# Moving one group of matmuls earlier in TensorE's order, and cutting another into single blocks, in a two-layer transformer kernel

## Chip, cores and metric

The kernel runs on one core of a Trainium2 chip. The metric is the device time of one execution in microseconds (us), the median of the runs. The engines of a core are TensorE (PE in the profile; its weight loads are PEld), VectorE (DVE), ScalarE (ACT), GpSimd (POOL) and SyncE (SP), which here issues the DMAs.

## The reference

Two transformer blocks with adaptive layer norm, on x of 8 batch elements x 512 tokens x 128 channels. The change lies in the attention of the second block (16 heads of width 8). What is computed there, shortened:

```python
qkv = (x @ w_qkv.T + b_qkv)                      # q, k, v: [B, H, T, 8]
std_logits = einsum('bhqd,bhkd->bhqk', q, k) * scale
write_lines = exterior(w1, w2); read_lines = exterior(r1, r2)   # 6 numbers per token and head
incidence = einsum('bqhp,bkhp->bhqk', read_lines, J_write)
weights = decays[:, None, None] ** diffs_pos[None] * past[None]
logits = std_logits + incidence * weights[None] * bias_scale
logits = where(causal_mask, -inf, logits)        # key after query: out
attn = softmax(logits); out = einsum('bhqk,bhkd->bqhd', attn, v)
return out @ w_out.T + b_out
```

## The kernel before, in words

The program runs as stages: preparation, attention and feed-forward of block 0, then `attention1` (the function `attention1` holds all that the change touches; 491 to about 1015 us of the span), then the feed-forward of block 1.

In `attention1` there are 8 x 16 = 128 heads, numbered n. The 512 tokens are NT = 4 tiles of 128, so the causal scores of a head are 4 blocks on the diagonal and 6 below it (key tile k before query tile a). Every head is computed twice. First with queries on the partitions, only to find the largest score of each query; then, LAG = 8 heads later (j = n - 8), with keys on the partitions, with the maxima subtracted through three more rows of the operands, and these scores go through the exponential and on to the product with v. The rows QO (queries) and KA (keys, with decay), KB, KC (for the diagonal) lie in SBUF in a ring of four groups of four heads and come from DRAM scratch by DMA.

Each engine runs its own loop over n = 0 ... 151, and the order within a turn ("slot") is written out by hand. TensorE's turn:

1. `on_diagonal(n)` (L1299, L1300, and the mask matmul L1301), after VectorE's `weigh(n)`
2. in three slots of four (n mod 4 = 1, 2, 3, from head 13 on) `values` of an earlier group of four heads (L1356, fp32, 32 columns of the array each), in the fourth `turn_out` (L1364, transposes); once per batch element `turn_rows` and `project` (L1377, L1383)
3. `incidences_by_key(j)` (L1316): eight matmuls of 64 columns into bank psDT, after s_expd of head j-1
4. `side(n)`: a step of the operands of a later batch element (L1079 to L1115), in most slots
5. `below(n)` (L1308): the blocks below the diagonal into psX, after VectorE has read the maxima of head n-1 (s_rc)
6. `incidences(n+1)` (L1292) into psD
7. `on_diagonal_by_key(j)` (L1323 to L1325), after VectorE's `weigh_by_key(j)`
8. `below_by_key(j+1)` (L1333): six matmuls of 128 columns; every fourth slot `turn_maxima` (L1340)

VectorE's turn: `weigh(n)` (L1436, after L1292), `largest_below(n-1)` (L1454, L1455), `largest_on_diagonal(n)` (L1446, after L1301), `weigh_by_key(j)` (L1441, after L1316), `normalise` (L1467, L1471) every fourth slot, `residual` (L1478) once per batch element, then a step of its side work (L1121 to L1154). ScalarE's turn: a side step, copies of the output (L1575, every fourth slot), the exponentials of the diagonal (L1562, L1563, after L1325; the second signals s_expd), and those below it (L1557, after L1333).

The maxima of a head are gathered in mo, 4 x 4 numbers per partition: one row of four for each query tile, filled as far as there are blocks. L1460 takes the largest of each row of four.

Of the kernel before, what the change touches and what calls it, by code (L numbers as in the profile page):

```python
# [11 lines left out]
ALU = mybir.AluOpType  # L12
AX = mybir.AxisListType

P = 128
B, T, D = 8, 512, 128
NT = T // P
# [14 lines left out]
def tiles(ap, n=NT):  # L32
    return ap.rearrange("p (t c) -> p t c", t=n)


def over(ap, n):
    return ap.rearrange("p (o c) -> p o c", o=1).to_broadcast([ap.shape[0], n, ap.shape[1]])
# [12 lines left out]
class Chip:  # L50
# [9 lines left out]
    def sb(self, name, cols, dt=F32, rows=P, at=None):  # L60
        return (at or self.ctx).enter_context(self.nc.sbuf_tensor(name, [rows, cols], dt))[:, :]
# [799 lines left out]
def attention1(c, t, sh):  # L861
# [5 lines left out]
    nc, pe, dve, act, pool, sp, bank = c.nc, c.pe, c.dve, c.act, c.pool, c.sp, c.bank  # L867
    own = ExitStack()
    with own:
        sb = lambda *a, **k: c.sb(*a, at=own, **k)  # L870
        SCALE = float(DH) ** -0.5
        NR, KX = NL * H, T * (NT - 1) // 2
# [3 lines left out]
        HEADS, G, RING, LAG, NV = B * H, 4, 4, 8, 3  # L876
# [9 lines left out]
        HB = P // 2  # L886

        PAIRS = [(k, a) for k in range(NT) for a in range(k + 1, NT)]

        ROW_AT = {3: 0, 1: 512, 2: 512 + P}  # L890
        NP = len(PAIRS)
        SEG = NT + NP
        MAX_UNIT = 2.0 ** 15
        off = [P * a * (a - 1) // 2 for a in range(NT + 1)]
# [10 lines left out]
        s_inc, s_wq, s_own, s_ra, s_off, s_rb, s_rc, s_mx = c.signals("3", "inc wq own ra off rb rc mx")  # L905
# [23 lines left out]
        QO = [sb(f"QO{i}", G * T, dt=F16) for i in range(RING)]  # L929
        KB = [sb(f"KB{i}", G * T, dt=F16) for i in range(RING)]  # L930
        KC = [sb(f"KC{i}", G * T, dt=F16) for i in range(RING)]
        KA = [sb(f"KA{i}", G * KX, dt=F16) for i in range(RING)]
# [7 lines left out]
        mo = [sb(f"mo{i}", G * NT * NT) for i in range(2)]  # L940
# [10 lines left out]
        psD, psX, psDT, psXT, psO, psA = bank[0], c.banks(1, 2), bank[3], c.banks(4, 2), bank[6], bank[7]  # L951
# [9 lines left out]
        def place(n):  # L961

            return n // G % RING, n % G

        def group_at(n, after):

            q, r = divmod(n - after - G - LAG, G)
            return q if r == 0 and 0 <= q < GROUPS_ else None
# [8 lines left out]
        def rows_at(n, after):  # L977
            return next((b for b in range(B) if rows_slot(b) + after == n), None)
# [293 lines left out]
        def on_pe():  # L1272
            def block(x, n, a):

                i, h = place(n)
                return x[i][:, h * T + a * P:h * T + (a + 1) * P]
# [18 lines left out]
            def on_diagonal(n):  # L1295
                pe.wait_ge(s_wq, n + 1)
                for a in range(NT):
                    q, k = block(QO, n, a), block(KB, n, a)
                    pe.matmul(psD[HB:P, a * P:(a + 1) * P], q[:, HB:P], k, start=False, stop=False, skip_group_check=True)  # L1299
                    pe.matmul(psD[0:HB, a * P + HB:(a + 1) * P], q[:, 0:HB], k[:, 0:HB], start=False, stop=False, skip_group_check=True)  # L1300
                pe.matmul(tiles(psD), sh.identh, over(maskq, NT), start=False, stop=True, skip_group_check=True).then_inc(s_own, 1)  # L1301

            def below(n):
                if n:
                    pe.wait_ge(s_rc, n)
                i, h = place(n)
                for a, at in ROW_AT.items():
                    m = pe.matmul(psX[:, at:at + a * P], block(QO, n, a), KA[i][:, h * KX + off[a]:h * KX + off[a + 1]], start=True, stop=True, skip_group_check=True)  # L1308
                m.then_inc(s_off, 1)

            def incidences_by_key(n):
                if n:
                    pe.wait_ge(s_expd, n)
                for a in range(NT):
                    for z in HALVES:
                        m = pe.matmul(psDT[z, a * P:a * P + HB], block(KC, n, a)[:, z], block(QO, n, a)[:, z], start=a == 0, stop=False, skip_group_check=True)  # L1316
                m.then_inc(s_incT, 1)
# [24 lines left out]
            def values(q, k):  # L1342

                b = q // 4
                if k == 0:
                    pe.wait_ge(s_expd, G * (q + 1))
                    pe.wait_ge(s_expo, G * (q + 1))
                    if q:
                        pe.wait_ge(s_O, q)
                at, first = k * P, NT + sum(NT - 1 - x for x in range(k))  # L1350
                for c0, c1, e0 in ((at, at + P, at), (at + P, T, first * P)):
                    if c0 < c1:
                        for n in range(G * q, G * q + G):
                            h = n % H
                            r, v0 = 32 * (h % 4), (k * H + h) * VH
                            m = pe.matmul(psO[r:r + 32, c0:c1], vv[b % NV][:, v0:v0 + 32], ET[n % NE][:, e0:e0 + c1 - c0],  # L1356
                                          start=c0 == 0, stop=k == NT - 1, skip_group_check=True)
                if k == NT - 1:
                    m.then_inc(s_pv, 1)

            def turn_out(q):
                pe.wait_ge(s_oS, q + 1)
                for i in range(NT):
                    m = pe.transpose(psO[:, i * P:(i + 1) * P], oS[:, i * P:(i + 1) * P], sh.ident)  # L1364
                m.then_inc(s_oT, 1)

            def turn_rows(b):
                pe.wait_ge(s_O, 4 * b + 4)

                if b + 3 < B:  # L1370
                    pe.wait_ge(s_cp, 2 * (b + 3) + 2)
                else:
                    pe.wait_ge(s_rawlo, 2 * B)
                if b:
                    pe.wait_ge(s_Y, b)
                for i in range(NT):
                    m = pe.transpose(psA[:, i * P:(i + 1) * P], O[:, i * P:(i + 1) * P], sh.ident)  # L1377
                m.then_inc(s_OT, 1)
# [15 lines left out]
            for n in range(LAST):  # L1394
                j = n - LAG
                if n < HEADS:
                    on_diagonal(n)
                q = group_at(n, 1)
                if q is not None:
                    values(q, 0)  # L1400
                q = group_at(n, 2)
                if q is not None:
                    values(q, 1)
                q = group_at(n, 3)
                if q is not None:
                    values(q, 2)
                    values(q, 3)
                q = group_at(n, 4)
                if q is not None:
                    turn_out(q)  # L1410
                b = rows_at(n, 0)
                if b is not None:
                    turn_rows(b)
                b = rows_at(n, 1)
                if b is not None:
                    project(b)
                if 0 <= j < HEADS:
                    incidences_by_key(j)
                side(n)
                if n < HEADS:  # L1420
                    below(n)
                if n + 1 < HEADS:
                    incidences(n + 1)
                if 0 <= j < HEADS:
                    on_diagonal_by_key(j)
                if 0 <= j + 1 < HEADS:
                    below_by_key(j + 1)
                g, x = divmod(n - 5, G)
                if x == 0 and 0 <= g < GROUPS_:
                    turn_maxima(g)  # L1430

        def on_dve():
# [10 lines left out]
            def largest_on_diagonal(n):  # L1443
                g, x = divmod(n, G)
                dve.wait_ge(s_own, n + 1)
                dve.tensor_reduce(tiles(mo[g % 2][:, x * NT * NT:(x + 1) * NT * NT])[:, :, NT - 1], tiles(psD), AX.X, ALU.max).then_inc(s_ra, 1)  # L1446

            def largest_below(n):
                g, x = divmod(n, G)
                to = mo[g % 2][:, x * NT * NT:(x + 1) * NT * NT]  # L1450
                dve.wait_ge(s_off, n + 1)


                dve.tensor_reduce(to[:, 12:15], tiles(psX[:, 0:3 * P], 3), AX.X, ALU.max).then_inc(s_rb, 1)  # L1454
                dve.tensor_reduce(to[:, 6:11:2], tiles(psX[:, 512:512 + 3 * P], 3), AX.X, ALU.max).then_inc(s_rc, 1)  # L1455
                if x == G - 1:
                    dve.wait_ge(s_rc, n + 1)
                    if g >= 2:
                        dve.wait_ge(s_split, 5 * (g - 1))
                    dve.tensor_reduce(mx[g % 2], tiles(mo[g % 2], G * NT), AX.X, ALU.max).then_inc(s_mx, 1)  # L1460
# [73 lines left out]
            for n in range(LAST):  # L1534
                j = n - LAG
# [126 lines left out]

        on_sp()
        on_pe()
        on_dve()
        on_act()
# [324 lines left out]
```

## Time and profile before

| | |
|---|---|
| median of 3 runs | 1245.75 us (1245.54 to 1246.93) |
| the profiled execution | 1245.75 us, of which the span 1244.5 us |
| TensorE matmul busy in the span | 913.2 us (73%), 9743 matmuls |
| VectorE, ScalarE, GpSimd busy | 808.8 (65%), 573.3 (46%), 383.1 us (31%) |
| mean granted TensorE clock | 0.856 of full speed |

A row of the timeline has start, duration, engine, line, what it writes and reads, and in brackets how long the engine was idle before it and who released it. In the chain of waits a piece's duration is what it adds to the chain. Matmuls overlap, so one that lasts 0.22 us may add 0.03. Start and duration are in us.

### The profile page before, as it was taken

Reading aid. Unit: us, or ns where it says so; the run is one execution under the profiler, and the core shown is the slowest. Engines: PE = TensorE matmul, PEld = TensorE weight load, DVE = VectorE, ACT = ScalarE, POOL = GpSimd, SP = SyncE. Lnnn points to the kernel's source line nnn. Section 1 sums busy time; section 2 is a strip of 40 time slices with the busy share of each in tenths; the row PEclk is TensorE's granted clock in tenths of the full one; section 3 lists DMA queues with packets and bytes.
Section 4 is the critical chain, followed back from the end, with each engine's and each line's share of the span. In section 5 each row is a group of like instructions: output and inputs, shape, how many; then the busy total and the mean of one; then the engine's idle time right before and its main releaser. Section 6 shows DMA issues by size and latency. Waiting matters only on the chain.

```text
span 1244.5 us, 24906 instructions
## 1 busy us (share of the span) xinstructions
PE 913.2 (73%) x9743; PEld 560.9 (45%) x9743; DVE 808.8 (65%) x1873; ACT 573.3 (46%) x1044; POOL 383.1 (31%) x638
## 2 busy tenths in 40 slices
PE   3778753575663125698989898989999951989888
PEld 1344422353442013365656565656666630344344
DVE  4554537889886712778686867686777617665754
ACT  2333322232221202266656565666565642768766
POOL 0121222444432154544444536263621100011000
PEclk8898986767686555599999999999999985999999
DMA  3000000000000116152525252434342111000000
GB/s 102 9 0 1 1 19 0 1 0 1 1 0 14 45 45 161 44 154 57 154 48 138 60 146 58 129 81 109 101 106 63 28 54 40 1 18 10 9 18 18
DMA packets 70575, 63.56 MB, mean 51 GB/s; under 512 B 30492, under 2 KB 62716, under 8 KB 70456
## 3 DMA queue, kind: packets, MB, share of 16 engines
q1 hardware_dynamic: 69016, 60.59, 18.4%
q8 instruction: 81, 1.33, 0.5%
q10 hardware_dynamic: 1440, 1.33, 0.4%
q14 instruction: 38, 0.31, 0.1%
HBM read 34.02 MB, written 27.36 MB: 49 GB/s over the span
## 4 chain that ended last, share of the span: by engine, by line
PE 49%; DVE 14%; issue 10%; POOL 6%; ACT 4%; SPq 1%; DMA 1%; POOLq 0%; ACTq 0%; DVEq 0%
PE bank L1788 10%; PE bank L1356 6%; PE bank L1301 3%; PE bank L1308 3%; PE bank L1299 3%; PE bank L1333 2%; PE bank L1316 2%; PE bank L689 2%; PE bank L1292 2%; PE bank L690 2%; PE bank L1325 2%; PE bank L1323 1%; PE bank L1101 1%; ACT 4g L1853 1%; DVE 4f L1903 1%
## 5 line engine op out<-in xcount | busy, mean ns | idle before, releaser
L1562 ACT ACTIVATE ET<-bank 64x512 f32<-64x512 f32 x128 | 75.5, 590 | 107.3 <-PE bank L1325 107.3
L1788 PE MATMUL bank<-act,h 128*128 128x512 f16 x512 | 113.1, 382 | 0.0
L1557 ACT ACTIVATE ET<-bank 128x768 f32<-128x768 f32 x128 | 103.1, 805 | 3.5 <-PE bank L1333 1.2
L1890 DVE TENSOR_TENSOR act<-4f,act 128x512 f16<-128x512 f32 x96 | 66.4, 691 | 56.8 <-ACT act L1843 56.6
L1436 DVE TENSOR_TENSOR bank<-bank,W 128x256 f32<-128x256 f32 x128 | 54.8, 428 | 72.3 <-PE bank L1292 72.3
L1441 DVE TENSOR_TENSOR bank<-bank,WT 128x256 f32<-128x256 f32 x128 | 55.2, 431 | 62.9 <-PE bank L1316 62.9
L1446 DVE TENSOR_REDUCE mo<-bank 128x4 f32<-128x512 f32 x128 | 88.1, 688 | 9.7 <-PE bank L1301 4.7
L1356 PE MATMUL bank<-ET,vv 128*32 128x128 f32 (+2 forms) x1792 | 90.9, 329 | 0.8 <-DVE O L1471 0.8
L1299 PE MATMUL bank<-KB,QO 128*64 128x128 f16 x512 | 55.0, 233 | 42.2 <-DVE bank L1436 42.2
L1788 PEld LDWEIGHTS bank<-act,h 128*128 128x128 f16 x512 | 50.4, 99 | 60.5 <-issue 2.3
L1843 ACT ACTIVATE act<-4f 128x512 f16<-128x512 f32 x96 | 60.4, 629 | 27.7 <-DVE 4f L1903 25.7
L1454 DVE TENSOR_REDUCE mo<-bank 128x3 f32<-128x384 f32 x128 | 70.0, 547 | 0.0
L1455 DVE TENSOR_REDUCE mo<-bank 128x3 f32<-128x384 f32 x128 | 70.0, 546 | 0.0
L1308 PE MATMUL bank<-KA,QO 128*128 128x384 f16 (+2 forms) x384 | 66.8, 285 | 0.0
L136 POOL TENSOR_TENSOR rstd<-ve,neghalf 128x4 f32<-128x4 f32 x16 | 18.2, 1136 | 155.9 <-DVE ve L118 155.9
L1333 PE MATMUL bank<-QO,KA 128*128 128x128 f16 x768 | 64.4, 220 | 0.0
L1299 PEld LDWEIGHTS bank<-KB,QO 128*64 128x64 f16 x512 | 33.5, 113 | 55.2 <-DVE bank L1436 47.8
L1323 PE MATMUL bank<-QO,KB 128*64 128x128 f16 x512 | 51.7, 224 | 4.4 <-DVE bank L1441 4.2
L1333 PEld LDWEIGHTS bank<-QO,KA 128*128 128x128 f16 x768 | 54.1, 99 | 1.6
L1356 PEld LDWEIGHTS bank<-ET,vv 128*32 128x32 f32 x1792 | 44.6, 111 | 22.5 <-issue 20.7
L479 ACT ACTIVATE E<-bank,nm 128x512 f32<-128x512 f32 x32 | 22.0, 688 | 68.8 <-DVE nm L434 68.8
L1301 PE MATMUL bank<-maskq,identh 128*128 128x512 bf16 x128 | 52.5, 410 | 0.0
(315 smaller groups left out, 2309.7 us busy)
## 6 DMA issues: line engine op xcount, KB each, us to landing
QO<-scr_q SPq DMA_DIRECT2D x32, 324.0 KB
KA<-scr_a SPq DMA_DIRECT2D x32, 252.0 KB
KB<-scr_k SPq DMA_DIRECT2D x32, 168.0 KB
scr_a<-dk SPq DMA_DIRECT2D x8, 288.0 KB, 2.6
KC<-scr_k SPq DMA_DIRECT2D x32, 72.0 KB
X<-in_x SPq DMA_DIRECT2D x8, 256.0 KB, 6.5
scr_q<-std SPq DMA_DIRECT2D x8, 256.0 KB, 2.4
scr_k<-std SPq DMA_DIRECT2D x8, 256.0 KB, 2.7
```

Source lines behind the costliest of these rows:

```text
L1299: pe.matmul(psD[HB:P, a * P:(a + 1) * P], q[:, HB:P], k, start=False, stop=False, skip_group_check=True)
L1301: pe.matmul(tiles(psD), sh.identh, over(maskq, NT), start=False, stop=True, skip_group_check=True).then_inc(s_own, 1)
L1308: m = pe.matmul(psX[:, at:at + a * P], block(QO, n, a), KA[i][:, h * KX + off[a]:h * KX + off[a + 1]], start=True, stop=True, skip_group_c ...
L1333: m = pe.matmul(psXT[:, x * P:(x + 1) * P], decayed(n, k, a), block(QO, n, a), start=True, stop=True, skip_group_check=True)
L1356: m = pe.matmul(psO[r:r + 32, c0:c1], vv[b % NV][:, v0:v0 + 32], ET[n % NE][:, e0:e0 + c1 - c0], start=c0 == 0, stop=k == NT - 1, skip_gro ...
L1446: dve.tensor_reduce(tiles(mo[g % 2][:, x * NT * NT:(x + 1) * NT * NT])[:, :, NT - 1], tiles(psD), AX.X, ALU.max).then_inc(s_ra, 1)
L1454: dve.tensor_reduce(to[:, 12:15], tiles(psX[:, 0:3 * P], 3), AX.X, ALU.max).then_inc(s_rb, 1)
L1455: dve.tensor_reduce(to[:, 6:11:2], tiles(psX[:, 512:512 + 3 * P], 3), AX.X, ALU.max).then_inc(s_rc, 1)
L1557: act.activation(ET[n % NE][:, T:SEG * P], psXT[:, 0:NP * P], ACT.Exp).then_inc(s_expo, 1)
L1562: act.activation(to[0:HB, :], psDT[0:HB, :], ACT.Exp)
L1788: m = pe.matmul(to, l, r, start=n == 0, stop=n == len(todo) - 1)
L1890: dve.tensor_tensor(lo, f32_[f % 3], hi, ALU.subtract).then_inc(s_lo, 1)
```

## The change

`incidences_by_key(j)` is issued directly behind `on_diagonal(n)`, ahead of the values, the transposes and the projection, and no longer behind them. `below(n)` issues six matmuls of 128 columns, one for each block, in an order of its own (BY_ROW), instead of three of 384, 128 and 256 columns; the first four fill one PSUM bank and the last two half of the next. `largest_below` reduces 512 and 256 columns instead of 384 and 384, and the maxima go to other places within a row of mo.

```diff
@@ -886,8 +886,7 @@
         HB = P // 2
 
         PAIRS = [(k, a) for k in range(NT) for a in range(k + 1, NT)]
-
-        ROW_AT = {3: 0, 1: 512, 2: 512 + P}
+        BY_ROW = [(0, 2), (1, 2), (0, 3), (1, 3), (0, 1), (2, 3)]
         NP = len(PAIRS)
         SEG = NT + NP
         MAX_UNIT = 2.0 ** 15
@@ -1303,9 +1302,8 @@
             def below(n):
                 if n:
                     pe.wait_ge(s_rc, n)
-                i, h = place(n)
-                for a, at in ROW_AT.items():
-                    m = pe.matmul(psX[:, at:at + a * P], block(QO, n, a), KA[i][:, h * KX + off[a]:h * KX + off[a + 1]], start=True, stop=True, skip_group_check=True)
+                for x, (k, a) in enumerate(BY_ROW):
+                    m = pe.matmul(psX[:, x * P:(x + 1) * P], block(QO, n, a), decayed(n, k, a), start=True, stop=True, skip_group_check=True)
                 m.then_inc(s_off, 1)
 
             def incidences_by_key(n):
@@ -1395,6 +1393,8 @@
                 j = n - LAG
                 if n < HEADS:
                     on_diagonal(n)
+                if 0 <= j < HEADS:
+                    incidences_by_key(j)
                 q = group_at(n, 1)
                 if q is not None:
                     values(q, 0)
@@ -1414,8 +1414,6 @@
                 b = rows_at(n, 1)
                 if b is not None:
                     project(b)
-                if 0 <= j < HEADS:
-                    incidences_by_key(j)
                 side(n)
                 if n < HEADS:
                     below(n)
@@ -1443,16 +1441,14 @@
             def largest_on_diagonal(n):
                 g, x = divmod(n, G)
                 dve.wait_ge(s_own, n + 1)
-                dve.tensor_reduce(tiles(mo[g % 2][:, x * NT * NT:(x + 1) * NT * NT])[:, :, NT - 1], tiles(psD), AX.X, ALU.max).then_inc(s_ra, 1)
+                dve.tensor_reduce(tiles(mo[g % 2][:, x * NT * NT:(x + 1) * NT * NT])[:, :, 0], tiles(psD), AX.X, ALU.max).then_inc(s_ra, 1)
 
             def largest_below(n):
                 g, x = divmod(n, G)
-                to = mo[g % 2][:, x * NT * NT:(x + 1) * NT * NT]
+                to = tiles(mo[g % 2][:, x * NT * NT:(x + 1) * NT * NT])
                 dve.wait_ge(s_off, n + 1)
-
-
-                dve.tensor_reduce(to[:, 12:15], tiles(psX[:, 0:3 * P], 3), AX.X, ALU.max).then_inc(s_rb, 1)
-                dve.tensor_reduce(to[:, 6:11:2], tiles(psX[:, 512:512 + 3 * P], 3), AX.X, ALU.max).then_inc(s_rc, 1)
+                dve.tensor_reduce(to[:, 2:4, 1:3], psX[:, 0:T].rearrange("p (a k c) -> p a k c", a=2, k=2), AX.X, ALU.max).then_inc(s_rb, 1)
+                dve.tensor_reduce(mo[g % 2][:, x * NT * NT + 5:x * NT * NT + 16:10], tiles(psX[:, T:NP * P], 2), AX.X, ALU.max).then_inc(s_rc, 1)
                 if x == G - 1:
                     dve.wait_ge(s_rc, n + 1)
                     if g >= 2:
```

The functions that it calls were there before: `decayed(n, k, a)` is a block of 128 columns of KA, `block(x, n, a)` one of QO, KB or KC.

## Rows read from the trace of the kernel before

**Rows 1.** Stretches (busy us and count of each engine, clock, DMA); one wait.

```profile
core 0: us, PE busy (x) PEld busy (x) DVE busy (x) ACT busy (x) POOL busy (x), PEclk, DMA share, GB/s
525.00:985.00 460.00, 427.75 (x7162) 283.69 (x7163) 344.63 (x803) 283.65 (x516) 193.66 (x409) 0.99 0.37 97
...
PEld bank L1299 <- DVE bank L1436: 45.8, 30, 4.3
```

**Rows 2.** Groups by line (count, busy us, mean ns, idle before), 480 to 1010.

```profile
L1446 DVE TENSOR_REDUCE mo<-bank 128x4 f32<-128x512 f32 x128 | 88.1, 688 | 9.7 <-PE bank L1301 4.7
...
L1454 DVE TENSOR_REDUCE mo<-bank 128x3 f32<-128x384 f32 x128 | 70.0, 547 | 0.0
...
L1441 DVE TENSOR_TENSOR bank<-bank,WT 128x256 f32<-128x256 f32 x128 | 55.2, 431 | 62.9 <-PE bank L1316 62.9
...
L1333 PEld LDWEIGHTS bank<-QO,KA 128*128 128x128 f16 x768 | 54.1, 99 | 1.6
```

**Rows 3.** Chain that ended last, 700 to 721 us: start, piece, what.

```profile
701.08 1.00 PE bank L1356 x16
702.09 0.24 PE bank L1316 x8
702.33 0.43 PE bank L1308 x3
...
703.49 0.34 PE bank L1333 x6
...
704.37 0.32 PE bank L1301
...
720.51 0.33 PE bank L1308 x3
```

**Rows 4.** Timeline of one slot, 700 to 704.7 us (heads 53 and 54).

```profile
700.12 0.59 ACT L1562 ACTIVATE ET<-bank 64x512 f32<-64x512 f32 x1 [1.02 <-PE bank L1325]
...
700.69 0.39 PE L1301 MATMUL bank<-maskq,identh 128*128 128x512 bf16 x1
700.72 0.38 ACT L1563 ACTIVATE ET<-bank 64x256 f32<-64x256 f32 x1
...
702.37 0.43 DVE L1441 TENSOR_TENSOR bank<-bank,WT 128x256 f32<-128x256 f32 x1 [0.56 <-PE bank L1316]
...
704.12 0.38 ACT L1563 ACTIVATE ET<-bank 64x256 f32<-64x256 f32 x1
...
704.31 0.39 PE L1301 MATMUL bank<-maskq,identh 128*128 128x512 bf16 x1
```

**Rows 5.** Heads 9 and 11, without values: chain at 529, timeline at 535.

```profile
529.01 0.25 PE bank L1316 x8
...
534.91 0.39 PE L1301 MATMUL bank<-maskq,identh 128*128 128x512 bf16 x1
...
535.38 0.32 PE L1316 MATMUL bank<-QO,KC 128*64 128x64 f16 x8
```

**Rows 6.** Timeline of VectorE and TensorE in the slot of head 50.

```profile
691.62 0.43 DVE L1441 TENSOR_TENSOR bank<-bank,WT 128x256 f32<-128x256 f32 x1 [0.34 <-PE bank L1316]
...
694.32 0.24 PE L1299 MATMUL bank<-KB,QO 128*64 128x128 f16 x1 [1.25 <-DVE bank L1436]
```

**Rows 7.** Timeline, slot of head 64, with the projection and the residual.

```profile
748.78 0.43 DVE L1441 TENSOR_TENSOR bank<-bank,WT 128x256 f32<-128x256 f32 x1 [0.84 <-PE bank L1316]
...
750.69 0.24 PE L1299 MATMUL bank<-KB,QO 128*64 128x128 f16 x1 [0.46 <-DVE bank L1436]
```

**Rows 8.** Timeline, slot of head 54: VectorE's side work on the decayed rows.

```profile
706.96 1.08 DVE L1148 TENSOR_TENSOR sq<-bank,Dk 96x128 f32<-96x128 f32 x3 [0.76 <-ACT raw L1200]
```

**Rows 9.** Timeline in the drain, after the last head by query.

```profile
1004.38 0.24 PE L1323 MATMUL bank<-QO,KB 128*64 128x128 f16 x1 [0.53 <-DVE bank L1441]
```

**Rows 10.** Stretches: the same four slots in two batch elements.

```profile
638.98:654.40 15.42, 11.80 (x185) 7.95 (x189) 11.75 (x33) 10.29 (x21) 5.70 (x11) 0.89 0.22 48
704.70:718.68 13.98, 10.36 (x185) 7.09 (x189) 11.66 (x33) 10.29 (x21) 5.70 (x11) 1.00 0.25 58
```


## The prediction

> **What bounds the kernel now.** I began with the table of stretches [rows 1]: from 525 to 985 us TensorE is busy for 427.75 of 460 us at a granted clock of 0.99, VectorE for 344.63. So TensorE has no room in this stage, VectorE has. The groups by line [rows 2] then show what invites the change: VectorE stands idle for 62.9 us ahead of its 128 `weigh_by_key` (L1441), always until TensorE's L1316. Idle time of an engine that isn't the bound costs nothing, so I followed the chain of waits through one turn of the loop ("slot" n, from the mask matmul L1301 of head n to that of head n+1). In an ordinary slot the chain never leaves TensorE [rows 3]: L1301 0.32, values 1.00, `incidences_by_key` 0.24, `below` 0.43, ..., `below_by_key` 0.34, and on to the next head. Such a slot gets shorter only if TensorE does less; it gets longer with every wait that TensorE gains.
>
> I read all 128 starts of L1301 in the timeline. From head 16 on the pattern repeats about every 16 slots. In the waits, TensorE waited 30 times in 500 to 1000 us for `weigh` (L1436) [rows 1]; 24 of these lie after head 13, in four kinds of slot that the last part of VectorE's side work ends: heads 18, 34, ..., 98 (the norms of the lines), 32, 48, ..., 112 (the residual), and 22 and 23, 38 and 39, ... (the decayed rows). Five more (21, 37, ..., 85: the layer norm's statistics) are late by only 0.2 us. All others are TensorE's.
>
> **What the change moves.** Two edits, almost independent.
>
> *`incidences_by_key(j)` goes from behind the values to directly behind `on_diagonal(n)`.* It waits for s_expd, the end of ScalarE's L1563 on head j-1, because it writes the PSUM bank that L1562 and L1563 read. Today the values (1.00 us in this slot) or the transposes stand between, and this wait is covered. Without that cover, by this slot's times: L1562 starts 700.12, L1563 ends 700.72 + 0.38 = 701.10; L1301 ends 700.69 + 0.39 = 701.08 [rows 4]. ScalarE finishes just when TensorE would start, and TensorE's next instruction starts before that end, since instructions overlap in its pipeline (values after L1301: chain position 701.08). In the timeline L1563 ends 0.01 to 0.06 us after L1301 in every slot that TensorE sets (head 53's row stands for them). It is so by construction: ScalarE needs 0.59 + 0.38 us and two handovers after L1325, TensorE has 0.34 + 0.34 + 0.32 to do.
>
> The trace of before even shows the new order. Heads 9 to 12 have no values yet, so there L1316 follows L1301 directly [rows 5]. Where ScalarE wasn't late (the slot at 528.69), L1316's work ends 0.25 after L1301's, at 529.26 against 529.01. At 534.91 it had to wait: L1301 ends 535.30, L1316 starts 535.38 and ends 535.70, 0.40 later. The same at the two neighbours (0.38). The wait costs 0.13 to 0.14 us a slot; I take 0.135. Everything queued behind it on TensorE is late by it: values, side matmuls, `below`, `incidences(n+1)`, `on_diagonal_by_key`, and with it ScalarE's next exponentials, so the phase between the two engines reproduces itself and no later slot gets the time back.
>
> Slots 13 to 127 are 115. Four kinds don't pay: heads 18, 34, ... 98 (VectorE ends the slot, and doesn't wait for L1316 now), and 19, 23 and 24 and their repeats (TensorE got to L1301 so late that ScalarE was long done), 6 each. 115 - 24 = 91, times 0.135 = **+12.3 us**.
>
> Gains, in the slots that VectorE ends. L1441 now starts as soon as L1446 is done.
> - Norms (head 50): L1441 was idle 0.34, TensorE then waited 1.25 [rows 6]. All 0.34 come off: 6 x 0.34 = 2.0.
> - Residual (head 64): L1441 idle 0.84, TensorE's wait 0.46 [rows 7]. The wait goes wholly, about 0.5 with the restart of the pipeline: 6 x 0.5 = 3.0.
> - Statistics (head 53): L1441 idle 0.56 [rows 4], L1301 of head 54 ends 0.20 after L1563 (704.70 against 704.50) [rows 4]: 5 x 0.2 = 1.0.
> - Decayed rows (heads 54 and 55): VectorE isn't held by L1441 but 0.76 for ScalarE's copy L1200 [rows 8], which waits for the side transposes; these keep their place. Nothing.
>
> Sum **-6.0**. With both kinds together the trade is poor: the idle time of VectorE is 62.9 us, but only 6 of it stands on the path.
>
> In the drain (heads 120 to 127 by key, no new rows) TensorE today waits 0.53 for L1441 after L1316 [rows 9]. The values now cover that. But TensorE instead stands after `below_by_key` until the exponentials are done: 0.59 + 0.38 and two handovers of 0.05 is 1.07 behind L1325, less 0.34 of `below_by_key`: 0.73. Net +0.2 in the six slots with values, about 0 in the two with transposes, where it already waits for ScalarE: **+1.2**.
>
> *`below(n)` in six matmuls of 128 columns instead of 384 + 256 + 128.* The columns stay 768. Three matmuls behind a full-width matmul take 0.33, six in L1333, same shapes and types, 0.34 [rows 3]: the extra weight loads are covered. At most 0.01 x 128 = 1.3, at least 0: **+0.6**.
> Here the Trainium skill ("TensorE: Matmul & The Clock Gate", section "Back-to-back issue gap") says that a sustained stream of load and matmul pairs runs at about 81 ns for a pair of 128 columns, because both operations set the spacing. Six pairs would then take 0.49 us; the trace doesn't bear it out, with 0.34 for six (56 ns each).
>
> The maxima are taken over 512 + 256 instead of 384 + 384 columns. 688 ns for 512 and 547 for 384 [rows 2] is 141 for 128 more, so 406 for 256: 688 + 406 = 1094 against 2 x 547 = 1094. Nothing; and VectorE would have to hold the slot for it to count. The new places in mo change only addresses.
>
> *Changes of array tiling.* `below` starts 0.10 later behind the 64-column matmuls than behind full-width ones (0.43 against 0.33 [rows 3]). Before: full, 32 (values), 64 (L1316), full. After: full, 64, 32, full. Three changes each; with transposes two each. I book 0. What no row shows is 64 to 32 and 32 to full; the nearest rows allow -0.10 to +0.10 for them, in about 90 slots: -9 to +9 us, kept for the range.
>
> **Sum.** 12.3 - 6.0 + 1.2 + 0.6 = +8.1. The profiled execution took 1245.75 us (span 1244.5 and 1.25 outside it), which is also the median. 1245.75 + 8.1 = 1253.8 us.
>
> **Rivals.**
> A. *The wait stays cheap and VectorE's relief decides: faster.* For it: VectorE's idle 62.9 us, and gains of 6.0 that are solid. It decides from a wait below (6.0 - 1.2 - 0.6)/91 = 0.046 us a slot. With no wait at all, 1245.75 - 4.2 = 1241.5. Against it: three slots of this very trace pay 0.13 to 0.14.
> B. *Near balance, within 0.2%:* the wait costs 0.03 to 0.07, or the clock helps. In three of the six slots with the long wait of 2.3 to 2.7 us TensorE came back at a lower clock: 15.42 us at 0.89 against 13.98 at 1.00 for the same slots, heads 38 to 41 and 54 to 57 [rows 10]. The three cost about 4 us in all. If none happens after the change, -4: 1249.6; if all six, +4: 1258. Alone it doesn't reach no change; with a tiling term of -0.05 it does.
> C. *The new order costs array time.* If 64 to 32 columns costs 0.10 more than a change costs now, 90 x 0.10 = +9, so 1263. If the loads of `below` set its pace (99 ns each, L1333's [rows 2]), six take 0.59 instead of 0.33: +0.26 in some 100 slots, +26, 1280. Against the first: the equal count of changes. Against the second: the same six pairs of L1333 in 0.34 [rows 3].
> By the skill's 81 ns (page named above) the second would be 0.49 - 0.33 = 0.16 a slot, an estimate of +16 us and 1270.
> D. *The change does nothing:* the maxima and sizes of work are the same, and if TensorE had slack in the ordinary slots, both effects would vanish, 1245.75. The chain without a gap [rows 3] speaks against it.
>
> **Numbers.** Forecast (slower by 3 to 12 us) 0.67; C 0.12; A 0.11; B within 0.2% and D together 0.10. About 0.2% (2.5 us) is what a measurement of this kernel can tell from no change. Faster 0.11, same 0.10, slower 0.79. The forecast's own range is 1249 to 1258: 0.13 against 0.14, and the clock. To hold 8 in 10 I go down to 1245, the balance, and up to 1262, near the first case of C.
>
> **What would show it.** Profile after: L1441's idle time falls from 62.9 to under 20; a new idle time ahead of `incidences_by_key` until ScalarE's L1563, about 90 times; L1563's end and L1316's start 0.05 apart; ordinary slots longer by 0.13 (between two L1301); norm slots shorter by 0.3; `below` 0.34 to 0.44 in the chain. It would be wrong if ScalarE got to L1562 earlier than 0.3 us behind L1325's start, if an ordinary slot grew by under 0.05, or if `below`, with its twelve instructions, took over 0.5.

## The result, and the profile after

The changed kernel takes 1253.44 us (median of 8 runs) against 1245.78 us (8 runs): +7.7 us, ratio 1.0065, 95% interval 1.0047 to 1.0083. That is slower, and by clearly more than the 0.2% that separates from no change; forecast were 1253.8 us and 0.79 for slower. The profiled execution after the change has a span of 1251.6 us (1244.5 before).

The groups by line of the changed kernel, whose line numbers are a little lower (L1439 is `weigh_by_key`, L1434 `weigh`, L1306 `below`, L1450 and L1451 its maxima, L1314 `incidences_by_key`, L1559 ScalarE's second exponential, L1300 the mask matmul); they answer to [rows 2]:

```profile
L1434 DVE TENSOR_TENSOR bank<-bank,W 128x256 f32<-128x256 f32 x128 | 55.0, 430 | 119.0 <-PE bank L1291 119.0
...
L1450 DVE TENSOR_REDUCE mo<-bank 128x4 f32<-128x512 f32 x128 | 87.1, 680 | 1.1 <-PE bank L1306 1.1
L1306 PE MATMUL bank<-KA,QO 128*128 128x128 f16 x768 | 68.0, 228 | 0.0
...
L1439 DVE TENSOR_TENSOR bank<-bank,WT 128x256 f32<-128x256 f32 x128 | 54.2, 423 | 15.3 <-PE bank L1314 15.2
...
L1451 DVE TENSOR_REDUCE mo<-bank 128x2 f32<-128x256 f32 x128 | 53.2, 416 | 0.0
```

Of the kernel before, `weigh` in the groups by line, and the wait of `incidences_by_key` for ScalarE in 500 to 1000 us:

```profile
L1436 DVE TENSOR_TENSOR bank<-bank,W 128x256 f32<-128x256 f32 x128 | 54.8, 428 | 72.3 <-PE bank L1292 72.3
...
PEld bank L1316 <- ACT ET L1563: 2.6, 7, 0.6
```

The change does what it seems made for: VectorE's idle time ahead of `weigh_by_key` falls from 62.9 to 15.3 us. It comes back ahead of `weigh`, which waits for TensorE's `incidences(n+1)`: 119.0 us now, 72.3 before. VectorE was never what most slots waited for. The new wait of TensorE stands in the waits of the changed kernel, 500 to 1000 us (total, times, longest):

```profile
PEld bank L1314 <- ACT ET L1559: 39.6, 103, 0.9
PEld bank L1298 <- DVE bank L1434: 37.3, 24, 4.3
```

103 times it now waits for ScalarE, 7 times before, and 24 instead of 30 times for VectorE's `weigh` [rows 1]. One slot (head 53) in the timeline, to be laid beside [rows 4], and its chain beside [rows 3]:

```profile
700.75 0.39 PE L1300 MATMUL bank<-maskq,identh 128*128 128x512 bf16 x1
700.78 0.38 ACT L1559 ACTIVATE ET<-bank 64x256 f32<-64x256 f32 x1
701.21 0.20 PEld L1314 LDWEIGHTS bank<-QO,KC 128*64 128x64 f16 x8 [0.37 <-ACT ET L1559]
701.21 0.32 PE L1314 MATMUL bank<-QO,KC 128*64 128x64 f16 x8
```

```profile
700.78 0.39 ACT ET L1559
701.16 0.04 issue
701.21 0.32 PE bank L1314 x8
701.52 1.00 PE bank L1354 x16
702.52 0.44 PE bank L1306 x6
```

The mask matmul ends 701.14, the exponential 701.16, the weights of L1314 start 0.05 behind it. ScalarE has entered a chain that was TensorE's alone. L1314 adds 0.32 to it instead of 0.24.

To see all slots at once, I took the starts of the mask matmul of every head in both timelines and subtracted neighbours. The distances repeat to 0.01 or 0.02 us, so a table by kind of slot says nearly all (us; the last column is of `after_one_exp`, explained under "Take the wait away"):

| slot of head | before | after | without second exp., after's order |
|---|---|---|---|
| 107, 115, ... values, no side | 3.18 / 3.19 | 3.29 / 3.30 | 3.15 / 3.16 |
| 17, 65, 97: values, no side | 3.40 / 3.41 | 3.51 / 3.52 | 3.37 / 3.38 |
| 20, 52, 116: transposes, no side | 2.83 / 2.84 | 2.99 / 3.00 | 2.84 / 2.85 |
| 26, 58, 90: values and side | 4.10 | 4.24 / 4.25 | 4.10 |
| 31, 63, 95: turn_rows | 3.77 / 3.78 | 3.78 / 3.79 | 3.64 |
| 18, 50, 98: norms (VectorE's) | 4.51 | 4.08 | 4.08 |
| 32, 64, 96: residual (VectorE's) | 4.26 | 3.88 | 3.74 |
| 21, 53, 85: statistics | 3.61 | 3.51 | 3.37 |

### The profile page after: what moved, and what is told of

The parts are those of the page before. It is cut to its first block, busy times and chain, and to the rows that moved or that the text cites. A ratio compares the mean times of both kernels' runs of the same rounds, so it can differ in the third digit from the quotient of the medians.

```text
span 1251.6 us, 25674 instructions
## 1 busy us (share of the span) xinstructions
PE 918.1 (73%) x10127; PEld 578.5 (46%) x10127; DVE 803.2 (64%) x1873; ACT 573.2 (46%) x1044; POOL 383.1 (31%) x638
## 4 chain that ended last, share of the span: by engine, by line
PE 42%; issue 14%; DVE 13%; ACT 8%; POOL 6%; DMA 1%; SPq 1%; POOLq 0%; ACTq 0%; DVEq 0%
PE bank L1784 10%; PE bank L1354 5%; PE bank L1306 3%; ACT ET L1559 3%; PE bank L1314 3%; PE bank L689 2%; PE bank L1291 2%; PE bank L690 2%; PE bank L1323 2%; PE bank L1321 1%; PE bank L1100 1%; PE bank L1362 1%; ACT 4g L1849 1%; DVE 4f L1899 1%; POOL xq L574 1%
## 5 line engine op out<-in xcount | busy, mean ns | idle before, releaser
L1434 DVE TENSOR_TENSOR bank<-bank,W 128x256 f32<-128x256 f32 x128 | 55.0, 430 | 119.0 <-PE bank L1291 119.0
L1444 DVE TENSOR_REDUCE mo<-bank 128x4 f32<-128x512 f32 x128 | 88.3, 690 | 10.2 <-PE bank L1300 4.7
L1450 DVE TENSOR_REDUCE mo<-bank 128x4 f32<-128x512 f32 x128 | 87.1, 680 | 1.1 <-PE bank L1306 1.1
L1306 PE MATMUL bank<-KA,QO 128*128 128x128 f16 x768 | 68.0, 228 | 0.0
L1306 PEld LDWEIGHTS bank<-KA,QO 128*128 128x128 f16 x768 | 53.0, 102 | 28.5 <-issue 25.5
L1439 DVE TENSOR_TENSOR bank<-bank,WT 128x256 f32<-128x256 f32 x128 | 54.2, 423 | 15.3 <-PE bank L1314 15.2
L1451 DVE TENSOR_REDUCE mo<-bank 128x2 f32<-128x256 f32 x128 | 53.2, 416 | 0.0
L1300 PE MATMUL bank<-maskq,identh 128*128 128x512 bf16 x128 | 52.3, 408 | 0.0
```

The costliest lines, as they stand in the source:

```text
L1306: m = pe.matmul(psX[:, x * P:(x + 1) * P], block(QO, n, a), decayed(n, k, a), start=True, stop=True, skip_group_check=True)
L1450: dve.tensor_reduce(to[:, 2:4, 1:3], psX[:, 0:T].rearrange("p (a k c) -> p a k c", a=2, k=2), AX.X, ALU.max).then_inc(s_rb, 1)
```

## The experiments

**One edit at a time.** `split_only` has the second edit alone, `move_only` the first:

```diff
 # move_only
                 if n < HEADS:
                     on_diagonal(n)
+                if 0 <= j < HEADS:
+                    incidences_by_key(j)
...
-                if 0 <= j < HEADS:
-                    incidences_by_key(j)
                 side(n)
```

> Only the second edit: `below` in six matmuls, maxima over 512 + 256 columns; `incidences_by_key` stays behind the values. Account of the prediction: +0.6 us, at most +1.3, so 1245.8 to 1247.1 us, and the six matmuls take 0.43 or 0.44 in the chain of an ordinary slot, as the three did. Rival (the six weight loads show): most of the +7.7 us of the whole change is here, about 1253 us, with `below` at 0.5 us or more in the chain.

Measured: 1245.90 us against 1245.99, ratio 0.9994 (0.9983 to 1.0006). One slot in its chain of waits:

```profile
702.66 0.25 PE bank L1314 x8
702.91 0.44 PE bank L1306 x6
```

Six matmuls add 0.44 where three added 0.43. The slots are 0.00 to 0.01 us longer. The weight loads are covered; the rival falls.

> Only the first edit: `incidences_by_key` directly behind `on_diagonal`, `below` in three matmuls. Account of the prediction: the whole loss is here, +7 us, 1252.8 us (1251 to 1255), with about 100 waits of `incidences_by_key` for ScalarE's second exponential. Rival (weight loads): at most 1246.5 us. If the two edits hinder each other, this one and the split alone don't add up to +7.7.

Measured: 1249.41 us, ratio 1.0029 (1.0014 to 1.0043). Slower, but by 3.4 us where I expected 7, and the two edits don't add up to 7.7. Slot by slot the trace of `move_only` is that of the changed kernel, to 0.01 us, except around heads 54 to 57, 71 to 73 and 86 to 87, and slot 111. It had 105 waits for ScalarE. So something other than the order of work also moved the medians, which the next runs take up.

**Early only where VectorE ends the slot.**

```diff
+        FIRST = [H * b + 2 for b in range(1, 7)] + [H * b for b in range(2, 8)] + [H * b + 5 for b in range(1, 6)]
...
                 if n < HEADS:
                     on_diagonal(n)
+                if n in FIRST:
+                    incidences_by_key(j)
...
-                if 0 <= j < HEADS:
+                if 0 <= j < HEADS and n not in FIRST:
                     incidences_by_key(j)
```

> The kernel before, with `incidences_by_key` early in 17 slots alone, those that VectorE ends (heads 18, 34, ..., 98; 32, 48, ..., 112; 21, 37, ..., 85), late in all others. Account of the prediction, with the slot times of the two traces: 6 x 0.43 + 6 x 0.38 + 5 x 0.10 = 5.4 us less than before, 1240.4 us (1238 to 1243, the clock included), and no more than 11 exposed waits for ScalarE's second exponential. Rival (VectorE's relief is worth nothing in itself, and the slots were only shifted by the clock): within 1 us of before.

Measured: 1245.53 us, ratio 0.9988 (0.9977 to 0.9998): hardly anything. Yet in the trace the 17 slots are all shorter as forecast (4.07, 3.88, 3.51 us). (It waits for ScalarE 24 times between 500 and 1000 us, the kernel before 7 times: all 17 early slots do, not 11, but where VectorE ends the slot the wait is covered.) The gain was given back elsewhere. Here are the slots of heads 38 to 40, 54 to 56 and 86 to 88 in this kernel:

```profile
639.81:655.24 15.43, 11.81 (x185) 7.97 (x182) 11.69 (x33) 10.48 (x22) 5.31 (x10) 0.89 0.20 48
704.61:720.04 15.43, 11.81 (x185) 7.96 (x182) 11.68 (x33) 10.48 (x22) 5.30 (x10) 0.89 0.21 54
834.21:849.63 15.42, 11.80 (x184) 7.94 (x181) 11.67 (x33) 10.47 (x22) 5.29 (x10) 0.89 0.21 50
```

The same three slots of three batch elements, all at a granted clock of 0.89 and 15.4 us. In the kernel before one such stretch was at 0.89 and one at 1.00 ([rows 10], whose heading says four slots; from the mask matmul of head 38 to that of head 41 there are three). Summed over all such stretches, against their shortest kind, the profiled executions lost 4.2 us (before), 4.7 (after), 1.3 (`move_only`), 3.1 (`split_only`) and 8.2 (this kernel). So in the profiled executions the low clock gave back 4.0 of the 5.4 us. It isn't the whole: this execution, 1249.27 us, was the slowest of the twelve, and it also began `attention1` 1.2 us later than that of the kernel before and took 2.9 us longer behind it, at a mean granted clock of 0.874 against 0.894, both in stages that the edit doesn't touch. What the clock cost in the other executions of the median isn't known.

**The drain.** As the changed kernel, with the old order once n >= HEADS.

> The changed kernel, but in the drain (after the last head by query) `incidences_by_key` stays behind the values. The traces show the drain 1.5 us longer after the change. Account of the prediction: those 1.5 us come back, 1251.9 against 1253.4 us. Rival (the drain is set by ScalarE in either order): same as the changed kernel, 1253.4 us.

Measured: 1252.46 us; 1.0 less than the changed kernel, and its interval (1.0029 to 1.0055 of before) overlaps that one's, so the medians leave it open. The traces don't: from the last mask matmul to the last residual it takes 32.69 us, before 32.82, after the change 35.28. Of the changed kernel's extra 2.5, 1.5 are the drain proper, where it stands for ScalarE once a slot:

```profile
1003.92 0.32 PE L1314 MATMUL bank<-QO,KC 128*64 128x64 f16 x8 [0.74 <-ACT ET L1559]
```

and 0.9 are the last projection, L1381, 2.08 us for its eight matmuls against 1.16 (L1383) before. In `move_only`, with the same drain order, the whole took 34.35. The rows of the last projection are below, with the other observations on the clock.

**Keeping TensorE busy in the long wait.** At the end of six slots (22, 38, ..., 102) TensorE waits long for VectorE's work on the decayed rows: 2.28 us in five of them and 1.73 in the last. The kernel before, timeline at two of them and the stretch behind the first, at half the clock:

```profile
644.21 0.30 PE L1299 MATMUL bank<-KB,QO 128*64 128x128 f16 x1 [2.28 <-DVE bank L1436]
...
903.30 0.24 PE L1299 MATMUL bank<-KB,QO 128*64 128x128 f16 x1 [1.73 <-DVE bank L1436]
```

```profile
644.25:647.60 3.35, 3.35 (x44) 2.21 (x45) 1.91 (x4) 0.23 (x1) 3.11 (x4) 0.50 0.00 0
```

I put matmuls there whose result nobody reads, into the free half of psX's second bank, at the end of TensorE's turn in these slots (FILL holds 22, 38, ..., 102; its declaration and that of s_fill are left out):

```diff
+                if n in FILL:
+                    for _ in range(15):
+                        m = pe.matmul(tiles(psX[:, 6 * P:8 * P], 2), sh.identh, over(maskq, 2), start=True, stop=True, skip_group_check=True)
+                    m.then_inc(s_fill, 1)
...
                 dve.wait_ge(s_off, n + 1)
+                if n in FILL:
+                    dve.wait_ge(s_fill, FILL.index(n) + 1)
```

> The kernel before, with 15 matmuls of 256 columns (1.6 us at full clock, result unused) put into TensorE's long wait of 2.3 us at the end of slots 22, 38, ..., 102; VectorE reads the maxima of these heads after them. Theory (the low clock comes from this wait, and is what hides the slot arithmetic in the medians): no slot 23, 24, 39, 40, 55, 56, 71, 72 is longer than its shortest kind (5.96 and 5.01), 3 to 4 us less than before, 1242.3 us. Rival (the low clock is independent of the wait, a drift of the chip): the same number of slow slots and 1246 us or, for the added work, more.

Measured: 1240.64 us, ratio to before 0.9954 (0.9937 to 0.9971): 4.9 us faster for 90 matmuls more, where 3 to 4 were expected. In the traces the slots of heads 12 to 126 take 4.4 us less; the start of `attention1`, 2.8 us earlier, and the stages behind it, 1.9 us longer, lie outside what the edit touches. Timeline, and the stretch that answers to [rows 10] and to the three above:

```profile
639.16 1.80 PE L1435 MATMUL bank<-maskq,identh 128*128 128x256 bf16 x15
641.60 0.24 PE L1301 MATMUL bank<-KB,QO 128*64 128x128 f16 x1 [0.64 <-DVE bank L1442]
```

```profile
635.98:649.96 13.98, 12.00 (x199) 8.49 (x197) 11.66 (x34) 10.29 (x21) 5.31 (x10) 1.00 0.22 52
700.24:714.22 13.98, 12.00 (x199) 8.48 (x197) 11.67 (x34) 10.29 (x21) 5.31 (x10) 1.00 0.23 57
828.78:842.76 13.98, 12.00 (x199) 8.48 (x197) 11.66 (x34) 10.29 (x21) 5.31 (x10) 1.00 0.24 58
```

The idle time before `on_diagonal` is 0.64 instead of 2.28 us, the slot is as long as at the full clock before (5.96), and all three stretches run at the full clock, 2.4 GHz. In none of the traces of the four filled kernels (the other three follow) is one of these slots longer than its shortest kind: 0 of 24 places, against 27 of 48 in the eight traces without filling. The low clock (1.2 GHz) did come from the wait.

> The changed kernel with the same filling. Theory: 4 to 5 us less than the changed kernel, 1249 us, and a distance of 7 us (5.5 to 8.5) to the kernel before with filling: the exposed wait for ScalarE (12) less VectorE's relief (6) plus the drain (1.5). Rival (a good part of the +7.7 was the clock): the distance shrinks to under 5 us.

Measured: 1248.48 us (1245.51 to 1252.45), 5.0 less than the changed kernel. Its distance to the kernel before with filling is 7.8 us, without the clock's part in these slots in either; the rival, under 5 us, falls. The account of the prediction below shows what of it is the change's.

> Only the early `incidences_by_key`, `below` in three matmuls, with the filling. The traces show slot for slot the same lengths as with both edits, and 4.7 us of difference that lies in slots 55, 56, 58, 72, 74, 88 and 112. Theory (that difference is the clock and one late fetch): within 1 us of the changed kernel with filling, 1249 us. Rival (the split of `below` does cost once the move is made): 3 to 4 us less than it, 1245.5 us.

Measured: 1247.27 us, 1.2 under `after_filled`, and no longer 4.0 as the unfilled pair. In the traces the stretch from the mask matmul of head 12 to that of head 127 takes 447.11 and 448.11 us: 0.4 is slot 111 (a late fetch, below), the rest the split's 0.00 to 0.02 a slot. In the unfilled pair the same stretch differs by 4.7 us: 3.4 is the clock, 0.6 slot 111, 0.7 the rest. So the gap between `move_only` and the changed kernel was mostly clock, and the split costs about 0.6 us.

> `incidences_by_key` early in the 17 slots that VectorE ends, with the filling. Its trace without filling has every mechanical gain (5.6 us over the 17 slots) but six slow pairs of slots instead of three, 8.2 us against 4.2. Theory: the fastest of all, 5.5 us under the kernel before with filling, 1237 us (1235.5 to 1239.5). Rival (the relief only moves the wait into the next slots): equal to the kernel before with filling.

Measured: 1237.39 us, ratio to before 0.9929 (0.9904 to 0.9954): faster than the kernel before and the changed one, 3.3 us under `before_filled`, where I expected 5.5. The traces give 4.8 us over slots 12 to 126: -5.4 in the 17 slots, 0.0 in 97 others, +0.5 in slot 111. The rest of the difference to the medians isn't resolved (1237.39, from 1232.96 to 1241.51, against 1240.64, from 1239.71 to 1241.28; six runs each); the traces show `attention1` beginning 1.9 us later in the faster kernel, behind a stage that the edit doesn't touch.

**Take the wait away.** ScalarE's second exponential of the diagonal is left out in both orders (keys 64 to 127 of a diagonal block against the second half of the queries get weight zero), so ScalarE is done 0.4 us earlier (a changed `memset` that keeps these values at zero is left out here):

```diff
-                act.activation(to[0:HB, :], psDT[0:HB, :], ACT.Exp)
-                act.activation(half(to[HB:P, :], 1), half(psDT[HB:P, :], 0), ACT.Exp).then_inc(s_expd, 1)
+                act.activation(to[0:HB, :], psDT[0:HB, :], ACT.Exp).then_inc(s_expd, 1)
```

> The kernel before with ScalarE's second exponential of the diagonal (L1563, keys 64 to 127 of each tile) left out, s_expd signalled by the first; these values stay zero and the output is wrong for it. ScalarE is free 0.4 us earlier. Theory: the values cover the wait in this order, so the ordinary slots keep their lengths (3.19, 3.41, 4.10 us) and only the drain gets up to 1 us shorter: 1245 us. Rival (ScalarE's load as such is on the path): 2 us or more less.

Measured: 1248.69 us, 2.3 more than before, where 1245 was expected. The ordinary slots kept their lengths to 0.01 us, as expected. The drain looks unchanged (32.79), but up to the start of the last projection it is 0.5 us shorter (31.13 against 31.62), within the forecast; the projection then ran partly at the low clock, 1.63 us against 1.16. The excess lies where the edit doesn't reach: in the profiled execution the first mask matmul is 1.6 us later, the stages behind `attention1` take 3.2 us more, and the low clock in the long waits cost 5.3 us against 4.2. Heads 10 to 12, which have no values in front of `incidences_by_key`, lose 0.14 us each (3.45 to 3.31, 3.49 to 3.35): the slots from which the prediction took its price.

> The changed kernel with the same exponential left out. Theory (each ordinary slot pays 0.1 to 0.16 us because it waits for that exponential): all slots fall back, slots of 3.30 to 3.19 or less, 4.25 to 4.10, and the drain by 2 to 3 us. With VectorE's relief kept that is 5 to 7 us under the kernel before with the same cut, 1239 us. Rival (the loss is the array's: new changes of tiling, or six weight loads): the slots stay at 3.30, 3.51 and 4.25, 1252 us.

Measured: 1239.05 us, 14.4 less than the changed kernel; without that exponential the old order is no faster. The 1239 of the forecast is met, but partly by luck: the distance to the old order without that exponential is 9.6 us, not 5 to 7, and that kernel came out 3.7 above its forecast. The traces bear the 9.6 out: 8.4 in the slots (6.9 is VectorE's relief, which no new wait eats into here, the rest the changes of tiling less the six matmuls, both below) and 1.2 in the drain. Its slots are the last column of the table: the loss is gone wherever it was, and the waits for ScalarE fall from 103 to 13. Timeline:

```profile
697.83 0.39 PE L1300 MATMUL bank<-maskq,identh 128*128 128x512 bf16 x1
698.14 0.20 PEld L1314 LDWEIGHTS bank<-QO,KC 128*64 128x64 f16 x8 [0.23 <-issue]
698.15 0.32 PE L1314 MATMUL bank<-QO,KC 128*64 128x64 f16 x8
```

L1314 starts 0.07 before the mask matmul ends and waits for nobody. The rival (the array pays for the new order) predicted no change here, so it falls.

## Why the prediction was right, point by point

The mechanism was as forecast. The table sets the terms of the sum against what the traces of the filled kernels and of the one without the second exponential give (us; slots of heads 13 to 126 without slot 111, then the drain up to the last projection). The wait is `after_filled` less `after_one_exp`; the tiling term is what the new order without the wait leaves when VectorE's relief and the six matmuls are taken off.

| term | forecast | measured |
|---|---|---|
| exposed wait | +12.3 | +12.8 |
| VectorE's relief: norms | -2.0 | -2.6 |
| residual | -3.0 | -3.1 |
| statistics | -1.0 | -1.2 |
| changes of tiling | 0 | -2.1 |
| six matmuls | +0.6 | +0.6 |
| drain | +1.2 | +1.55 |
| sum | +8.1 | +6.0 |

*The exposed wait.* The price and the count are right: from the last column of the table of slots to the middle one every kind of slot that TensorE sets grows by 0.14 or 0.15 us (3.15 to 3.29, 3.37 to 3.51, 2.85 to 2.99, 4.10 to 4.24, 3.64 to 3.78), 89 slots in all (those of the residual and the statistics among them) where 91 were booked. It was in the trace of before, in heads 9 to 12 [rows 5]. As booked, heads 19, 23, 24 and their repeats don't pay.

*The changes of tiling.* Small, but not 0, and this is the term that was mis-sized most. The last column against the first is the new order without the wait: -0.03 in slots with values alone, +0.01 to 0.02 with transposes alone, -0.04 with transposes and side (head 28, 3.78 to 3.74), 0 with values and side, and -0.14 in the `turn_rows` slots. In these I had not counted: before, values, transposes, L1316 and `below` make four changes of tiling, after three. There the wait and this gain cancel (3.78 both). That the one change fewer makes the -0.14 is argued from the count, not tried; what makes the -0.03 wasn't tried either.

*VectorE's relief.* Norms -0.43 instead of -0.34 each (L1439 now starts 0.08 before L1444's end by the profile, so 0.34 was too small). Residual: -0.37 in the changed kernel, that is -0.51 and the new wait, as booked. Statistics -0.10, that is -0.24 and the wait. Decayed rows: nothing, as forecast, and they pay the wait at head 54. The long waits there, which I gave as 2.3 to 2.7 us, were 2.28 in five slots and 1.73 in the sixth.

*Drain.* TensorE stands 0.73 or 0.74 a slot for ScalarE where I worked out 0.73; of the six values from 1000 us on only the first is less, 0.57.

*Six matmuls:* about 0.6 between the filled kernels, nothing that `split_only`'s medians resolve. *Maxima, 0:* 680 + 416 = 1096 ns against 1094.

The mechanics so cost 6.0 us where the prediction said 8.1, and the measured +7.7 is nearer to 8.1 partly by luck. In the traces of the filled pair slots 12 to 126 give 5.4 us (73 longer slots +9.9, 17 shorter -5.3, 24 alike -0.1, slot 111 +0.9), the drain 1.5, the last projection 0.9, together 7.8. Slot 111 and the projection aren't the change's as far as the traces show. Slot 111 waits for the fetch of KA and took 3.77 to 5.84 us in the twelve traces, whatever the order; the projection ran at the low clock, which `move_only` with the same order in the drain didn't meet, filled or not. That the medians of the pair differ by 7.8 too is a coincidence: the two profiled executions are 11.7 us apart, because `attention1` begins 3.7 us later in `after_filled` and the stages behind it take 0.4 more. In the twelve traces that beginning (the first mask matmul) lies between 490.3 and 494.8 us, and the stages behind take 225.0 to 228.7, whatever the edit. Why they vary is left open. The medians alone give the price no more finely than that.

Rival C's 81 ns for a pair (the Trainium skill, "TensorE: Matmul & The Clock Gate", section "Back-to-back issue gap") doesn't hold for these six pairs: 0.44 with 0.10 of tiling change in it.

*The clock, rival B.* I took it as -4 to +4 around the 4.2 us of the kernel before. It reached as far: 1.3 to 8.2 us in the eight profiled executions without filling. That it can take most of a gain of 5.4 us (`early_in_17_slots`) I had not expected. Why one kernel meets it three times and another six, with the same waits, is left open; one profiled execution of each can't tell a kernel's habit from chance.

## What to carry to other kernels

Idle time of an engine ahead of an instruction isn't a reason to issue its producer earlier, unless that engine ends the slot: here 62.9 us of idle time held 6.9 us, and 5.3 where the new wait is paid. Before moving an instruction, read what its own wait is covered by now, and compare the ends of the two engines it will stand between; a wait that was exposed in a few early iterations shows the price. And where the order is right in some slots and wrong in others, choose by slot: the same move in 17 slots of 128 gains 4.8 us in the traces of the filled pair, in all slots it loses.

Compare slot lengths in the traces, not only medians, when a clock can change: it moved them by as much as the edit. And where a sum from the traces meets the difference of the medians, look whether the stages that weren't edited stood still.

## What the runs showed of the hardware

A wait of TensorE of 2.28 us (in the sixth place 1.73) was followed by a granted clock of 1.2 GHz in some executions of the same slot and not in others: 3 of 6 places before, 3 after, 1 in `move_only`, 2 in `split_only`, 6 in `early_in_17_slots`, 3 in `late_in_drain`, 4 and 5 in the two kernels without the second exponential, each for 0.4 to 2.1 us of lost time. With 1.6 us of matmuls in the wait, 0 of 24 places, and the kernel before gained 4.9 us by its medians, 4.4 by its slots.

The same eight matmuls of the last projection took 2.08 us at half the clock and 1.16 at the full one, after the same idle time of 0.69 us. The stretches after the change and before it (columns as in [rows 1]):

```profile
1023.88:1025.95 2.07, 2.07 (x8) 1.78 (x8) 0.00 (x0) 0.00 (x0) 0.00 (x0) 0.50 0.00 0
```

```profile
1017.12:1018.28 1.16, 1.16 (x8) 0.97 (x8) 0.00 (x0) 0.00 (x0) 0.00 (x0) 1.00 0.00 0
```

A matmul that restarts after a semaphore wait costs more than the producer is late. ScalarE was late by 0.02 us against the mask matmul's end, L1314 started 0.05 behind it, and without the wait it starts 0.07 before the mask matmul's end. The three make the 0.14 by which the slot grew. (In the chain the same 0.07 shows as 0.32 instead of 0.24 for L1314.)
